# First head of the second layer: scores of block 3 ahead of the turned tokens, weight products in two other banks, and a changed order on ACT and POOL

## The reference, cut to what matters

```python
# layer 1
q = einsum('bnq,eq->bne', layer_norm(x), Wq) + bq
k = einsum('bmk,ek->bme', layer_norm(ctx), Wk) + bk
v = einsum('bmk,ek->bme', layer_norm(ctx), Wv) + bv
y = x + einsum('bne,fe->bnf', softmax(q @ k^T) @ v, Wd) + bd
# layer 2, 8 heads
Q, K, V = heads(y @ Wq), heads(ctx @ Wk), heads(ctx @ Wv)
score = where(mask, Q @ K^T / sqrt(256), -inf)
out = layer_norm((softmax(score) @ V) @ Wo + y)
```

## Time and profile before

| | us |
|---|---|
| median of 3 runs | 507.09 (507.08 to 507.10) |
| profiled execution | 506.7 |
| its span, first to last instruction | 504.9 |
| granted clock of TensorE, mean | 0.994 |
| layer 1 with its end, the first head of layer 2 beside it | 0 to about 130 |

### The profile page before, as it was taken

One profiled execution on the slowest core, in us unless ns is written; L12 is line 12 of the kernel. 1 busy time (PEld: TensorE's weight loads), 2 busy tenths in 40 slices (PEclk: granted clock), 3 DMA queues, 4 the chain that ended last, 5 costly groups with the idle time before them and its releaser, 6 DMA issues.

```text
span 504.9 us, 7552 instructions
## 1 busy us (share of the span) xinstructions
PE 475.2 (94%) x2424; PEld 395.6 (78%) x2424; DVE 334.4 (66%) x681; ACT 291.6 (58%) x480; POOL 244.2 (48%) x151
## 2 busy tenths in 40 slices
PE   0999999989999999999999999999999999999992
PEld 0877777867878888888888888888888888788891
DVE  4999856466685657565856575567656765665467
ACT  4667377466665665665656565666656564656222
POOL 4636763546756372717172726363645453353004
PEclk9999999999999999999999999999999999999997
DMA  8413013658766656564747474747474745561002
GB/s 264 142 44 125 1 32 115 223 184 237 193 229 208 208 167 208 168 211 164 225 149 239 136 246 134 251 138 249 139 254 138 229 159 182 163 211 43 0 2 83
DMA packets 53974, 81.97 MB, mean 162 GB/s; under 512 B 5792, under 2 KB 43072, under 8 KB 53824
## 3 DMA queue, kind: packets, MB, share of 16 engines
q1 hardware_dynamic: 44992, 50.16, 34.1%
q10 hardware_dynamic: 8960, 31.54, 16.6%
HBM read 49.16 MB, written 32.51 MB: 162 GB/s over the span
## 4 chain that ended last, share of the span: by engine, by line
PE 80%; DVE 8%; ACT 4%; DMA 3%; issue 2%; SPq 1%; POOL 1%; DVEq 0%; ACTq 0%
PE ps_scores L611 29%; PE ps_o L635 6%; PE ps_o L641 6%; PE ps_o L636 6%; PE ps_o L640 6%; PE ps_o L637 6%; PE ps_task L561 3%; PE ps_task L560 3%; PE ps_task L559 3%; PE ps_out L559 2%; DMA ring<-in_weights_a 2%; PE ps_out L560 1%; PE ps_out L561 1%; PE ps_turn L627 1%; PE ps_out L720 1%
## 5 line engine op out<-in xcount | busy, mean ns | idle before, releaser
L506 POOL TENSOR_TENSOR probs_t_lo<-probs_t_lo,probs_t_hi 128x1024 fp32r<-128x1024 f32 (+1 forms) x75 | 146.3, 1963 | 175.9 <-ACT probs_t_hi L992 175.9
L992 ACT ACTIVATE probs_t_hi<-probs_t_lo 128x1024 fp32r<-128x1024 f32 (+1 forms) x75 | 64.6, 881 | 34.7 <-DMA probs_t_lo<-scratch 34.6
L611 PE MATMUL ps_scores<-key_hi,q_hi 128*128 128x512 f32 x144 | 57.9, 402 | 1.4 <-DVE neg_scores L1320 1.0
L635 PE MATMUL ps_o<-probs_t_hi,val_hi 128*128 128x512 f32 (+1 forms) x144 | 56.7, 393 | 1.5 <-issue 0.9
L1307 DVE RECIPROCAL row_inv<-row_sum 128x1 f32<-128x1 f32 x72 | 11.3, 159 | 70.1 <-PE ps_scores L611 68.2
L611 PE MATMUL ps_scores<-key_rem,q_lo 128*128 128x512 f32 x144 | 56.5, 393 | 0.3 <-DVE q_lo L1395 0.3
L611 PE MATMUL ps_scores<-key_lo,q_hi 128*128 128x512 f32 x144 | 56.7, 394 | 0.0
L611 PE MATMUL ps_scores<-key_rem,q_hi 128*128 128x512 f32 x144 | 56.6, 393 | 0.0
L611 PE MATMUL ps_scores<-key_hi,q_lo 128*128 128x512 f32 x144 | 56.5, 392 | 0.0
L636 PE MATMUL ps_o<-probs_t_lo,val_hi 128*128 128x512 f32 (+1 forms) x144 | 56.4, 392 | 0.0
L641 PE MATMUL ps_o<-probs_t_lo,val_rem 128*128 128x512 f32 (+1 forms) x144 | 56.4, 393 | 0.0
(11 more groups left out here) (247 smaller groups left out, 1099.7 us busy)
## 6 DMA issues: line engine op xcount, KB each, us to landing
probs_t_lo<-scratch SPq DMA_DIRECT2D x240, 128.0 KB, 3.0
scratch<-neg_scores ACTq DMA_DIRECT2D x30, 512.0 KB, 3.2
scratch<-probs ACTq DMA_DIRECT2D x30, 512.0 KB, 3.7
ring<-in_weights_a SPq DMA_DIRECT2D x9, 512.0 KB, 4.9
ring<-in_weights_b SPq DMA_DIRECT2D x9, 512.0 KB, 5.3
ring<-in_keys_t SPq DMA_DIRECT2D x4, 512.0 KB, 3.3
ctx_raw<-in_context SPq DMA_DIRECT2D x2, 768.0 KB, 9.3
ring<-in_context SPq DMA_DIRECT2D x16, 96.0 KB, 2.6
```

The source lines that it names most:

```text
L506: nc.gpsimd.tensor_tensor(pt_lo[b][:, t, k, :], pt_lo[b][:, t, k, :].bitcast(f32), moved_part(j, k).bitcast(f32), ALU.subtract).then_inc(m ...
L611: last = pe.matmul(ps_scores[:, n], left, right[:, n], start=(i == 0), stop=(i == len(passes) - 1))
L635: pe.matmul(o0, val_hi[b][:, kt, :], hi, start=(kt == 0), stop=False)
L992: act.activation(moved_part(j, k), pt_lo[b][:, t, k, :].bitcast(f32), ACT.Copy)\
```

## The change

TensorE, first head: scores of block 3 come first, then `turn_y(1)`, then tasks 2 and 3 (products of the a weights), then tasks 0 and 1 (queries). Before it was `turn_y(1)`, scores, tasks 0, 1, 2, 3. Tasks 2 and 3 go into the banks `ps_turn[0]` and `ps_turn[1]` and count on a semaphore of their own, `first_a_done`; `task_done` is made up by the last query product (3 counts). The queries wait for each half of the turned tokens by itself. Scores of block 4 wait for the parts of the queries where they use them (`task=`), not for all ahead. ACT: in block 3 the exponentials come ahead of fetched block 1 and of task 0, the spill moves between tasks 0 and 1; in block 4 the exponentials and task 4 come ahead of fetched block 2 and of the values. DVE: the minimum of block 3 comes ahead of `split_y(1)`, the splits of tasks 0 and 1 after `turn_blocks`. POOL: the split of block 3 comes ahead of that of the values. No arithmetic is added or removed.

```diff
--- before.py
+++ after.py
@@ -224,6 +224,8 @@
 
         def task_bank(task):
 
+            if isinstance(task, int) and task in (TASKS0 + 2, TASKS0 + 3):
+                return ps_turn[task - TASKS0 - 2]
             return ps_out if isinstance(task, int) and task < TASKS0 + 6 and task % 2 else ps_task
 
         def last_banks(half):
@@ -280,6 +282,7 @@
         outb_made = sem("outb_made")
         biased = sem("biased")
         task_done = sem("task_done")
+        first_a_done = sem("first_a_done")
         task_hi = sem("task_hi")
         task_free = sem("task_free")
         b_hi_made = sem("b_hi_made")
@@ -512,8 +515,8 @@
             split_moved(0, 1)
             split_weights(HI_OF[PC_B1], 0)
             split_moved(0, 2)
+            split_moved(0, 3)
             split_values(PC_V10, 1, (0,))
-            split_moved(0, 3)
             split_moved(0, 4)
             split_values(PC_V10, 1, (1,))
             split_moved(0, 5)
@@ -560,7 +563,7 @@
                 pe.matmul(dst, lh, rl, start=False, stop=False)
                 return pe.matmul(dst, ll, rh, start=False, stop=stop)
 
-            def absorb(task, m, width=DIM):
+            def absorb(task, m, width=DIM, done=task_done):
 
                 dst = task_bank(task)[:, 0:width]
                 for k in range(DT):
@@ -568,17 +571,19 @@
                     right = slice((DT + k) * DIM, (DT + k) * DIM + width)
                     last = three(dst, (w_hi[:, left], w_lo[:, left]), (w_hi[:, right], w_lo[:, right]),
                                  k == 0, k == DT - 1)
-                last.then_inc(task_done, 1)
-
-            def queries(task, b, m, chunks=False):
+                last.then_inc(done, 1)
+
+            def queries(task, b, m, chunks=False, ys=False, dones=1):
 
                 for k in range(DT):
                     if chunks:
                         pe.wait_ge(chunk_split, CHUNKS * b + k + 1)
+                    if ys:
+                        pe.wait_ge(y_split, DT * b + k + 1)
                     s, mv = slice(m * P, (m + 1) * P), slice(b * QUERIES, (b + 1) * QUERIES)
                     last = three(task_bank(task)[:, :], (a_hi[:, k, s], a_lo[:, k, s]),
                                  (xt_hi[:, k, mv], xt_lo[:, k, mv]), k == 0, k == DT - 1)
-                last.then_inc(task_done, 1)
+                last.then_inc(task_done, dones)
 
             def folded_queries(task, b):
 
@@ -846,12 +851,10 @@
             def first_body():
 
                 for j in range(2 * QT):
-                    if j == 3:
-                        turn_y(1)
                     if j == QT:
                         pe.wait_ge(piece_split, PC_KR1 + 1)
-                        pe.wait_ge(task_free, task_no(0, 2))
-                    if j > 0:
+                        scores(0, j, task=task_no(0, 0))
+                    elif j > 0:
                         scores(0, j)
                     else:
                         pe.wait_ge(piece_split, PC_KA0 + 1)
@@ -864,13 +867,14 @@
                         for t in range(QT, 2 * QT):
                             project(-1, t)
                     if j == 3:
-                        pe.wait_ge(y_split, 2 * DT)
-                        queries(task_no(0, 0), 1, 0)
-                        queries(task_no(0, 1), 1, 1)
+                        turn_y(1)
+
                         pe.wait_ge(piece_split, pieces_a(0))
+                        pe.wait_ge(pt_split, 16)
                         for m in range(2):
-                            pe.wait_ge(task_free, task_no(0, m + 1))
-                            absorb(task_no(0, m + 2), m, CTX)
+                            absorb(task_no(0, m + 2), m, CTX, done=first_a_done)
+                        queries(task_no(0, 0), 1, 0, ys=True)
+                        queries(task_no(0, 1), 1, 1, dones=3)
                     if j == 4:
                         pe.wait_ge(task_free, task_no(0, 4))
                         queries(task_no(0, 4), 0, 0)
@@ -1193,11 +1197,6 @@
                 for j in range(2 * QT):
                     if j == 3:
                         round_y(1)
-                        round_moved(0, 1)
-                        round_queries(task_no(0, 0), 1, 0, 1)
-                    if j == 4:
-                        round_moved(0, 2)
-                        round_values(PC_V10, 1, (0,))
                     if j == 5:
                         round_moved(0, 3)
                         move_remainder(task_no(0, 5), 0)
@@ -1211,18 +1210,25 @@
                         spill(0, 1)
                         round_outputs(-1, 1)
                     if j == 3:
+                        round_moved(0, 1)
+                        round_queries(task_no(0, 0), 1, 0, 1)
+                        spill(0, j)
                         round_queries(task_no(0, 1), 1, 1, 1)
+                        act.wait_ge(first_a_done, 2)
                         round_a(task_no(0, 2), 0, -1.0 / 16, CTX)
                         round_a(task_no(0, 3), 1, -1.0 / 16, CTX)
                     if j == 4:
                         round_queries(task_no(0, 4), 0, 0, 1)
+                        round_moved(0, 2)
+                        spill(0, j)
+                        round_values(PC_V10, 1, (0,))
                     if j >= 6:
                         keep_b(task_no(0, j), j - 6)
                     if j == 7:
                         spill(0, 7)
                     if j == 2 or j >= 6:
                         round_moved(0, j - 2)
-                    if j != 1 and j < 7:
+                    if j not in (1, 3, 4, 7):
                         spill(0, j)
                     if j == 3:
                         round_weights(ring_count(PC_B1), 0)
@@ -1622,21 +1628,20 @@
 
             def first_body():
                 for j in range(2 * QT):
-                    if j == 3:
-                        split_y(1)
                     minimum(0, j, 1)
                     if j == 2:
                         for t in range(QT, 2 * QT):
                             add(-1, t)
                     if j == 3:
-                        split_task(0, 0)
-                        split_task(0, 1)
+                        split_y(1)
                     if j == 5:
                         split_task(0, j)
                     turn_blocks(0, j)
                     if j == 1:
                         split_outputs(-1, 1)
                     if j == 3:
+                        split_task(0, 0)
+                        split_task(0, 1)
                         split_task(0, 2)
                         split_task(0, 3)
                     if j == 4:
```

## The result

The changed kernel takes 509.05 us (median of 6 runs, 508.22 to 510.63); the kernel before took 507.08 beside it. The ratio is 1.004 with a 95% interval of 1.0027 to 1.0054: slower, by 2.0 us, and above the range of the prediction, which ended at 508.5. So the change costs 0.8 to 2 us, 0.2 to 0.4%.

The account below looks back on a forecast made before the run. TensorE, busy 94% of the span, was taken as the bound. 1.55 us gained less 2.0 given back is 0.45 us slower: 507.15 by the profiled execution's own time, forecast 507.5, range 505.5 to 508.5.

Parts of the forecast that it names:

- part 4: POOL, SP, head 0: later values hold the weight load and block 4's fetch; TensorE stands 2.0 us before head 1's queries.
- the landing of the fetch: SP's fetch of block 4, last issue at 124.3: taken to land in 4.0 us, so ACT rounds block 4 at 128.35.
- the sum: Whole kernel: 1.55 us gained, 2.0 given back, 0.45 us slower; 507.15 by the profiled execution's own time, forecast 507.5.
- rival (b): Block 7, before batch 1's values: ACT's lateness passes through its spill and fetch, 0.9 us more, 508.4; chance 0.22.
- Parts 1 and 2: TensorE, first head: block 3's scores go first, second queries late by 0.6 us, block 4's scores end 1.75 us earlier.
- rival (a): Block 4's fetch is in time, rounded by 126.3, and all of 1.55 us stays: 505.55; chance 0.2.
- Part 3: ACT, block 4: fetched block 2 behind the exponentials and queries; 1.55 us of the gain left at block 7's scores.
- the bounds of the landing: Block 4's fetch: the range 506.1 to 508.1 us given to the forecast itself, chance 0.55.

Follow-up runs that it names:

- e1: Changed kernel with the fetch of block 4 ahead of the load of head 1's weights on SP's queue; 505.52 us, ratio 0.997 to the kernel before.
- e3: Changed kernel with the first half of batch 1's values rounded on ACT and split on POOL earlier, ahead of POOL's splits of blocks 2 and 3; 505.62 us.
- e6: Changed kernel with ACT's old order in block 4 and POOL's old order; 506.80 us, ratio 0.9990 to the kernel before.
- e2: Changed kernel with POOL's old order, the split of batch 1's first values ahead of that of block 3; 507.12 us, ratio 0.9996 to the kernel before.
- e4: Changed kernel run again without an edit, on another occasion; 507.88 us over 12 runs, ratio 1.0019 to the kernel before.
- e5: Kernel before with only POOL's swap, the split of block 3 ahead of that of the first values; 508.96 us, ratio 1.0031.
- e9: Changed kernel with the load of head 1's weights behind block 4's fetch, the wait for POOL's split kept ahead of the fetch; 506.55 us, ratio 0.9988.
- first set: The first 6 runs of the changed kernel, beside the kernel before; median 509.05 us, ratio 1.004.
- second set: The 12 runs of the unedited changed kernel on another occasion; 507.88 us, ratio 1.0019 to the kernel before.
- e7: Kernel before with one more wait on TensorE, ahead of head 1's queries until ACT has rounded block 5; 509.23 us, ratio 1.0034.

## Why the prediction was wrong

The mechanism was the right one and stood in part 4. What failed is the size of part 4: the landing of the fetch was taken as 4.0 us and was 4.7, the lateness handed on to block 7 (0.71 us) stood beside the sum and not in it, and the clock was not in the sum at all. On one clock (0.31 us added to the times of the changed kernel):

| step | forecast | measured |
|---|---|---|
| end of block 4's scores | 111.3 | 111.5 |
| gain where head 1's queries could start | 1.55 | 1.43 (scores begin at 127.45, 2.3 long) |
| POOL done with the values | 122.5 | 122.7 |
| load, fetch issued | 122.5, 123.0 | 122.7, 123.1 |
| landing of the fetch's fourth piece | 4.0 | 4.7 |
| ACT rounds block 4 | 128.35 | 129.2 |
| queries of head 1 start | 131.94 | 132.53 |
| more idle time at the values of batch 1 | 0, rival (b): 0.9 | 0.71 |
| a lower granted clock behind the idle time | not in the sum | in 7 of 18 runs |

- **Parts 1 and 2 held.** The scores, the turned tokens, the weight products in the other banks and the queries came within 0.2 us. e1 and e3 show the gain that is left when nothing eats it: 1.5 us (ratio 0.997), as rival (a) had priced it (505.55).
- **Part 3 held where it can be read.** Of the 1.6 us gained at the end of block 4's scores, 1.5 are left at block 7's, as foreseen. That the reorder on ACT is needed for it is not shown by a time: e6 undid POOL's order too, and against e2 it loses nothing.
- **Part 4, the term that was mis-sized: the landing.** I took 4.0 us for the last piece, between 3.8 and 4.1. It was 4.7. A part of this is a misreading: the figures of rows 8 are medians of the third and fourth piece, and what lets ACT go is the fourth, which alone took 4.0 and 4.2 where the rows have 3.8 and 4.1 (and 5.3 where I read 4.8 as the worst). The rest of the 0.7 is scatter that no run explains. The load just ahead, the spill of block 5 and the fetch of block 5 just behind meet in e4 and e5 too, and there the fourth piece took 4.4 and 4.1; in e9, with the same spill but no load in front, 3.0; in e2, with the spill issued between the pieces, 5.9. With 0.2 us of later issue this is 0.85 us at ACT. At TensorE it is 0.6 only, and that is luck: the steps from ACT's start to the queries took 3.3 us and not the 3.6 of the sum.
- **Rival (b) happened beside the forecast, not in place of it.** I gave it 0.22 as if it were another case, but it can follow whenever ACT is late, and then it adds to the same sum: the spill of block 7 left at 133.5 on the old clock (132.6 in (b)), took 5.3 to land as there, and block 7 was rounded at 144.6 (144.0 in (b)), with 0.76 us of waiting for its fetch. In the profiled run it cost 0.71 of the 0.9 priced. It doesn't follow each time. In e5 the spill of block 7 left at 133.88 (133.81 on the old clock), later than that, but landed in 4.2 us, and nothing was lost; in e4's profile, where TensorE was late for another reason, it cost nothing either. What it needs is a late ACT and a slow landing of that spill together.
- **What was not in the sum: the clock.** With both terms as measured (0.6 and 0.7 more) the sum is 508.8, or 508.45 from the profiled execution's 507.15; the runs of the first set at full clock took 508.22 to 508.65. The other 1 to 3 us come in some runs only, 7 of 18, and the median of the first set has half of them in it. I read the 2 us as if idle time cost only itself. The old profile had no idle time of that length between products, and its clock was at 1.00 through one of 0.91 us. But it did show, at its end, where TensorE has nothing left to do after 496.2, that idle time lets the clock fall (0.71, third number from the end):

```profile
498.00:500.00 2.00, 0.00 (x0) 0.00 (x0) 1.97 (x9) 0.00 (x0) 1.40 (x2) 0.71 0.20 68
```

- **The bounds.** The prediction calls 506.1 to 508.1 the bounds of the landing. By its own sum landings of 3.0 and 4.8 give 506.5 and 508.3.
- **The slack in e5.** The same error of method, once more: I moved a step on POOL without asking when its own input would be there.

What stays open: why the runs of the second set with a full clock (507.46 to 508.02) are 0.7 us faster than those of the first. The only profile of the second set, e4's, has the lower clock. An estimate from it: without the 1.7 us of the clock, the 0.9 behind 172.51 and the 0.9 between 450 and 480 us, and with some 0.2 us for block 7 (its fetch was down at 143.46, and ACT would have asked for it at 143.3), 510.88 becomes 507.6. This fits a second set in which the second idle time was mostly missing, but no profile at full clock shows it.

## What to carry to other kernels

A queue that serves transfers in order couples everything on it: before swapping two steps on a compute engine, look up which load waits for their count and what stands behind that load; here the cure was to put the urgent fetch first (e1), and the swap that seemed free cost 1.9 us by itself (e5). A lateness that is passed on to a spill or a fetch belongs in the sum of the next stage, with its chance, and not beside the sum as another case. Where several pieces release one step, the piece to price is the last one, not their median. And a new idle time on TensorE of about 2 us is priced with a risk of as much again.

## What the runs showed of the hardware

- After an idle time of 2.12 us (e4) and of 1.93 us (e7) the granted clock of TensorE fell to its lower level for 3 to 4 us in the profiled runs, in e4 with the first products, in e7 about 1 us behind the first, and products of 512 columns took 0.43 us each instead of 0.23. It is not so in each run: the changed kernel's profiled run had 2.30 us of idle time and a clock of 1.00 behind it, and of the 24 runs of the changed kernel and e7 8 show a lower mean clock. After 1.25 us (e5) and 0.91 us (before) no run shows it. The Trainium skill (TensorE: Matmul & The Clock Gate, Part 1) says that a monitor of the engine's activity passes half of the clock pulses when it was idle, and that the same kernel meets this differently from run to run; the two groups of e4 agree.
- The same fetch of 4 x 128 KB landed, by the median of its last two pieces, in 3.0 us with a load behind it (e9), in 4.0 (e5), 4.3 (e4) and 4.4 (changed) with the load in front, and in 5.7 with a load and a spill issued in the same microsecond (e2). I had expected no more than 4.8.
- A transfer on one queue slowed one on the other: a spill of 512 KB on ACT's queue landed in 5.3 us when a load of 512 KB had been issued on SP's queue 0.40 us before (e3), and in 2.6 us without one (e1).
